# A routed feed-forward layer whose first products split 192 features as 128 + 64, with the first steps and the late slots of an audio tower re-ordered

## The chip, the cores and the metric

The kernel runs on one NeuronCore of a Trainium2 chip, in one launch. The metric is the device time of that launch in microseconds (us). Three timed runs of the kernel before gave 555.41, 556.99 and 558.28 us; the median is 556.99 us.

## What is computed

The input is 64 audio clips of 4000 samples, in float32. Seven 1-D convolutions (128 channels each, strides 5, 2, 2, 2, 2, 2, 2), each followed by a layer norm over channels and a GELU, leave 12 tokens per clip. Then come a projection to 192 features, one attention block with 6 heads, and a feed-forward layer with 9 experts:

```
h = x[:, None, :]
for w, g, b, s in zip(conv_ws, ln_gs, ln_bs, strides):
    h = gelu(layernorm(conv1d(h, w, s)) * g + b)
h = layernorm(h) * fln_g + fln_b;  h = h @ proj_w + proj_b          # (64, 12, 192)
h = h + attention(layernorm(h))
xt = layernorm(h).reshape(-1, 192)                                  # 768 tokens
prob = softmax(xt @ Ws + bs);  p, route = max(prob), argmax(prob)
out_e = gelu(xt @ W1[e] + b1[e]) @ W2[e] + b2[e]                    # 192 -> 768 -> 192
final = out_0 if route == 0 else p * out_route + (1 - p) * out_0
h = h + final
```

Expert 0 is computed for every token (the "common" expert), and each token's own expert for tokens that are sorted by expert first.

## The kernel before

**The tower.** The clips are taken in 8 groups of 8 (`NT = 8`). A group's layer outputs are cut into chunks `(layer, group, k)`. For a chunk PE does the convolution (`conv`, L790 to L801), ACT squares (L1474), DVE sums the squares (L1176), POOL takes the power -1/2 (L647), DVE scales (L1185), PE turns the result (`turn`, L820) and ACT applies GELU with scale and offset by channel (L1492, L1504). The order is written out by hand: `SLOTS` is a list of rows (chunk, jobs, preparations), made of `HEAD`, five repeated bodies, `LAST` and `DRAIN`. Every engine walks through the slots in the same order and does its own part of each; `STEPS`, filled from the tables `RUN_0` to `RUN_7`, puts the steps of a token group (projection, attention, routing) into slots. Each engine executes strictly in its own order, so a slot's order decides what waits behind what.

**The start.** The first layer's norm needs no convolution output: the variance of a window follows from a 10 x 10 Gram matrix of the centred taps. So before the first convolution: PE centres the taps (L1000), DVE repeats them (L1310), PE makes the Gram products (L1008), DVE masks and adds them into `gram` (L1316, L1319). PE turns the samples ("raw", L838, copied by DVE, L1101), and multiplies them with `gram` ("z", L849 to L853); DVE makes the variances (L1108 to L1113), POOL takes their power -1/2 in four parts (L641, 2.4 us each), DVE scales the samples (`scale`, L1140 to L1149), PE turns them ("xt", L863), DVE copies (L1164), PE multiplies by the first taps ("l0", L874, with `w0t` from L1326 to L1335) and ACT applies GELU (L1515). The other layers' taps are centred and turned on PE in four batches of four (`turn_taps`, L769) and kept by ACT (L1466).

**The feed-forward layer.** The 192 features of a token lie on partitions as two halves of 96, with a row of ones as 97th row of the second half, which carries the bias `b1`. A job `("up", p, f)` multiplies one of six blocks of 128 hidden features of expert 0 with the tokens of part p (`PARTS`: 288, 288, 96, 96 tokens). `up_tile(j)` does the same for a tile of sorted tokens (L1057 to L1061):

```
for f in range(NF):
    o = ps[:, 2 * b + f // 4, (f % 4) * P:(f % 4 + 1) * P]
    nc.tensor.matmul(o, w[0:DH, 0, f * P:(f + 1) * P], xst[0:DH, b, 0, :], start=True, stop=False)
    last = nc.tensor.matmul(o, w[:, 1, f * P:(f + 1) * P], xst[:, b, 1, :], start=False, stop=True)
```

ACT applies GELU (L1521), and jobs `("down", i)` multiply by `W2` (L895). When the last group's experts are known (`rank`, L991 to L995, then the chain of small DVE operations from L1380 on), the sorted tokens are worked off in 13 tiles of 128 (`NTILE`): load, turn (L1048, L1049), copy (L1414), `up_tile` (L1060, L1061), GELU over all 768 hidden features (`hidden`, L1580), `down_tile` (L1072), result (L1425, L1431) and an indirect store (L751). The expert's first weights are copied out by ACT ahead of its tile (`pick`, L1585), alternately into `xhl` and `watt`. PE's order there is: turn tile j+2, up tile j+1, down tile j. The first weights of experts 1 to 8 are loaded after the last convolution into the space that the layers' outputs held (L587 to L591).

## Time and profile before

| | us |
|---|---|
| median of three runs | 556.99 |
| the profiled execution, as timed | 555.56 |
| its span in the trace | 553.8 |
| PE busy | 527.0 (95% of the span) |
| ACT busy | 307.0 (55%) |
| DVE busy | 306.1 (55%) |
| POOL busy | 257.3 (46%) |

A busy PE means only that a matmul was in flight, since matmuls are pipelined. A float32 product appears in the trace as two weight loads (PEld) and two matmuls (PE), called two passes below; a turn (transpose) is one pass. The time from one start to the next says what a pass costs, not its duration. The span is 1.76 us shorter than the time of the same execution.

### The profile page before, as it was taken

Reading aid. Unit: us, or ns where it says so; the run is one execution under the profiler, and the core shown is the slowest. Engines: PE = TensorE matmul, PEld = TensorE weight load, DVE = VectorE, ACT = ScalarE, POOL = GpSimd, SP = SyncE. Lnnn points to the kernel's source line nnn. Section 1 sums busy time; section 2 is a strip of 40 time slices with the busy share of each in tenths; the row PEclk is TensorE's granted clock in tenths of the full one; section 3 lists DMA queues with packets and bytes.
Section 4 is the critical chain, followed back from the end, with each engine's and each line's share of the span. In section 5 each row is a group of like instructions: output and inputs, shape, how many; then the busy total and the mean of one; then the engine's idle time right before and its main releaser. Section 6 shows DMA issues by size and latency. Waiting matters only on the chain.

```text
span 553.8 us, 11088 instructions
## 1 busy us (share of the span) xinstructions
PE 527.0 (95%) x4043; PEld 496.1 (90%) x4043; DVE 306.1 (55%) x759; ACT 307.0 (55%) x557; POOL 257.3 (46%) x298
## 2 busy tenths in 40 slices
PE   6899999999999999999999999999999996799995
PEld 6797998899999999999999999899899885699995
DVE  4665564457566676766575666745564443612231
ACT  1566647656584766568565846763663423544440
POOL 5674564776239426743762494333242120034433
PEclk9999999999999999999999999999999996999999
DMA  6490001693000000000000000000000088151110
GB/s 173 121 311 10 1 8 24 172 234 89 19 2 17 14 19 7 20 20 7 2 20 20 8 20 1 20 7 1 2 8 5 1 210 206 35 151 46 51 34 11
DMA packets 19495, 29.45 MB, mean 53 GB/s; under 512 B 2611, under 2 KB 13837, under 8 KB 19443
## 3 DMA queue, kind: packets, MB, share of 16 engines
q1 hardware_dynamic: 16131, 18.95, 13.1%
q0 software_dynamic: 3296, 9.78, 7.1%
q8 instruction: 34, 0.56, 0.4%
q14 instruction: 18, 0.15, 0.1%
q10 hardware_dynamic: 16, 0.00, 0.0%
HBM read 17.09 MB, written 9.18 MB: 47 GB/s over the span
## 4 chain that ended last, share of the span: by engine, by line
PE 86%; DVE 4%; ACT 3%; POOL 2%; issue 2%; SPq 1%; DMA 1%; POOLq 0%; DVEq 0%; ACTq 0%
PE ps L801 22%; PE ps L793 11%; PE ps L790 8%; PE ps L820 7%; PE ps L1072 5%; PE ps L874 4%; PE ps L1061 3%; PE ps L1060 3%; PE ps L895 2%; PE ps L791 2%; PE ps L795 2%; PE ps L940 2%; PE ps L963 2%; PE ps L949 1%; PE ps L863 1%
## 5 line engine op out<-in xcount | busy, mean ns | idle before, releaser
L647 POOL TENSOR_TENSOR rstd<-ssum,neghalf 128x4 f32<-128x4 f32 (+9 forms) x128 | 114.7, 896 | 199.5 <-DVE ssum L1176 199.3
L801 PE MATMUL ps<-wt,wide 128*120 128x128 f32 (+3 forms) x1200 | 144.6, 274 | 1.5 <-ACT wide L1504 1.2
L1474 ACT ACTIVATE work<-ps 128x512 f32<-128x512 f32 (+9 forms) x128 | 65.3, 510 | 139.1 <-PE ps L795 71.9
L801 PEld LDWEIGHTS ps<-wt,wide 128*120 128x120 f32 (+3 forms) x1200 | 138.0, 181 | 5.0 <-issue 2.7
L1185 DVE TENSOR_TENSOR work<-ps,rstd 128x512 f32<-128x512 f32 (+9 forms) x128 | 74.2, 579 | 67.0 <-POOL rstd L647 63.6
L1176 DVE TENSOR_REDUCE ssum<-work 128x4 f32<-128x516 f32 (+9 forms) x128 | 73.6, 575 | 64.4 <-ACT work L1474 64.1
L641 POOL TENSOR_TENSOR rstd<-var,half 128x12 f32<-128x12 f32 (+3 forms) x39 | 78.9, 2036 | 8.3 <-DVE var L1113 7.7
L1515 ACT ACTIVATE h<-ps,lncol 128x512 f32<-128x512 f32 (+1 forms) x120 | 80.5, 717 | 2.5 <-PE ps L874 2.4
L793 PE MATMUL ps<-wt,h 128*128 128x256 f32 x288 | 70.1, 380 | 0.0
L820 PE MATMUL ps<-ident,work 128*128 128x128 f32 (+3 forms) x408 | 64.1, 269 | 2.2 <-ACT wide L1492 1.0
L1492 ACT ACTIVATE wide<-ps,lncol 128x256 f32<-128x256 f32 (+1 forms) x112 | 54.4, 539 | 2.1 <-PE ps L820 1.8
L793 PEld LDWEIGHTS ps<-wt,h 128*128 128x128 f32 x288 | 51.1, 191 | 4.9
L790 PE MATMUL ps<-wt,h 128*128 128x128 f32 x400 | 54.7, 277 | 0.3 <-ACT h L1515 0.3
L820 PEld LDWEIGHTS ps<-ident,work 128*128 128x128 f32 (+3 forms) x408 | 47.6, 141 | 4.7 <-DVE work L1185 2.3
L790 PEld LDWEIGHTS ps<-wt,h 128*128 128x128 f32 x400 | 50.5, 192 | 1.3 <-issue 0.5
L874 PE MATMUL ps<-cols,w0t 128*128 128x512 f32 (+1 forms) x120 | 43.9, 421 | 2.6 <-ACT h L1515 1.5
L1504 ACT ACTIVATE wide<-ps,lncol 128x448 f32<-128x448 f32 (+4 forms) x64 | 41.9, 655 | 2.0 <-PE ps L820 1.2
L1580 ACT ACTIVATE work<-ps 128x768 f32<-128x768 f32 x13 | 10.5, 811 | 35.4 <-PE ps L1061 32.7
L1072 PE MATMUL ps<-W2s,work 128*128 x156 | 27.7, 327 | 0.0
L751 POOL DMA_INDIRECT out_dram<-xnat,idt x13 | 13.1, 1010 | 30.9 <-DVE xnat L1431 30.3
L1414 DVE COPY xst<-ps 96x256 f32<-96x256 f32 x13 | 5.5, 421 | 37.1 <-issue 19.3
L1072 PEld LDWEIGHTS ps<-W2s,work 128*128 128x128 f32 x156 | 25.0, 190 | 0.3 <-issue 0.3
(238 smaller groups left out, 813.2 us busy)
## 6 DMA issues: line engine op xcount, KB each, us to landing
sorted_tokens<-zero POOLq DMA_DIRECT2D x1, 5886.5 KB, 30.7
W2s<-in_L_ffn_W_dram SPq DMA_DIRECT2D x9, 576.0 KB, 8.2
wide<-in_L_ffn_W_dram SPq DMA_DIRECT2D x8, 576.0 KB
cols<-cols SPq DMA_DIRECT2D x24, 128.0 KB, 2.2
cols<-sorted_tokens SPq DMA_DIRECT2D x13, 96.5 KB, 2.2
xnat<-in_x_dram SPq DMA_DIRECT2D x7, 130.0 KB, 2.6
wt<-in_L_ffn_b_dram SPq DMA_DIRECT2D x1, 864.0 KB, 4.5
wide<-in_L_tok_conv_w_dram SPq DMA_DIRECT2D x4, 192.0 KB, 2.9
```

The costliest lines, as they stand in the source:

```text
L641: gp.tensor_tensor(rstd0[:, lo:hi], var0[:, lo:hi], half0[:, lo:hi], ALU.pow).then_inc(s_pow, 1)
L647: gp.tensor_tensor(rstd[0:rows, idx, 0:count], ssum[0:rows, idx, 0:count], neghalf[0:rows, 0:count], ALU.pow).then_inc(rstd_done, 1)
L790: nc.tensor.matmul(y[:, j * C:(j + 1) * C], local(2 * (lo + j) + 1), wt[:, 0, :], start=(j == 0), stop=False)
L793: nc.tensor.matmul(y[:, (j - 1) * C:(j + 1) * C], local(2 * (lo + j)), wt[:, 1:3, :].rearrange("p t c -> p (t c)"), start=False, stop=False)
L801: last = nc.tensor.matmul(y[0:rows, j * C:(j + 1) * C], h[l - 1][g % 2][:, at:at + rows], wt[:, TAP0[l] + tap, :], start=(tap == 0), stop= ...
L820: last = nc.tensor.transpose(to, xh[0:rows, n % 2, j * C:(j + 1) * C], ident[0:rows, 0:rows])
L874: nc.tensor.matmul(o[:, 0:w], w0t[:, j, :], xcol[(QUADS * g + q) % XC][:, 0:w], start=True, stop=True).then_inc(j_done, 1)
L1072: last = nc.tensor.matmul(o, ht[:, b, f * P:(f + 1) * P], W2s[:, bass.ds(own, 1), f, :].rearrange("p e d -> p (e d)"), start=(f == 0), sto ...
L1176: nc.vector.reduce_sum(ssum[0:rows, n % 4, 0:count], sq[0:rows, n % 2, 0:count, :], axis=X).then_inc(ssum_done, 1)
L1185: nc.vector.tensor_tensor(xh[0:rows, n % 2, 0:w].rearrange("p (j c) -> p j c", c=C), ybank(n)[0:rows, 0:w].rearrange("p (j c) -> p j c", c=C),
L1474: nc.scalar.activation(sq[0:rows, n % 2, 0:CUTS[l][k], 0:C], ybank(n)[0:rows, 0:w].rearrange("p (j c) -> p j c", c=C), ACT.Square).then_in ...
L1515: nc.scalar.activation(dst, src, ACT.Gelu, bias=lncol[:, 8:9], scale=lncol[:, 0:1]).then_inc(j_act, 1)
```

## The change

1. **Layout.** Of the 192 features, block f of the first half (f < 3) uses features 0 to 127 as one full product of 128 rows and features 128 to 191 as a product of 64 rows, which lie on partitions 64 to 127. Block f + 3 uses features 64 to 191 as the full product and 0 to 63, on partitions 0 to 63, as the product of 64 rows. The 64-row products of f and f + 3 follow each other and use different halves of the array and different PSUM banks. So six blocks take 6 full products and 3 pairs, where they took 12 products.
2. **Bias.** `b1` leaves the products. It is turned into columns once (`b1col`), and ACT adds it in the GELU. In the tiles, where a block's bias is a column of its own, the one GELU over 768 columns becomes six over 128; the picked weights have 1158 columns on 128 partitions where they had 1536 on 97. The routing bias `bs` is added by DVE, one more operation a group.
3. **Loads.** The first weights of each expert come in two loads, and two more bring the 64-row parts of all eight; the two one-partition loads of the bias go. Tap loads go ahead of the second load of samples.
4. **Start.** Gram products go ahead of the raw turn, `gram` ahead of its copy, the variance products ahead of the turned taps; the last two batches of taps are turned between the first steps of layer 0.
5. **Slots.** `up` jobs go in twos (f, f + 3); `LAST`, `DRAIN` and `RUN_5` to `RUN_7` are rewritten.

```diff
+DR = D - P
+NH2 = NF // 2
+HALF1 = DFF // 2
+WIDE1 = DFF + HALF1
+EW = WIDE1 + NF
...
 DRAIN = [
-    (None, [('up', 0, 0), ('up', 0, 1)], []),
+    (None, [('up', 0, 1)], []),
     ((2, 7, 0), [], []),
-    ((2, 7, 1), [], []),
+    ((2, 7, 1), [('up', 0, 0)], []),
...
+    (None, [('down', 1), ('down', 2)], []),
     (None, [('down', 0)], []),
...
-                nc.tensor.matmul(o[:, 0:(hi - lo) * M], W1c[0:DH, 0, f * P:(f + 1) * P], xt[0:DH, 0, cols], start=True, stop=False)
-                nc.tensor.matmul(o[:, 0:(hi - lo) * M], W1c[:, 1, f * P:(f + 1) * P], xt[:, 1, cols], start=False, stop=True)\
-                    .then_inc(j_done, 1)
+                w = (hi - lo) * M
+                nc.tensor.matmul(o[:, 0:w], W1c[:, f * P:(f + 1) * P], xt[:, f // NH2, cols], start=True, stop=False)
+                if f >= NH2:
+
+                    at = DFF + (f - NH2) * P
+                    nc.tensor.matmul(jbank(JOB[job] - 1)[:, 0:w], W1c[DR:P, at:at + P], xt[DR:P, 1, cols],
+                                     start=False, stop=True).then_inc(j_done, 1)
+                    nc.tensor.matmul(o[:, 0:w], W1c[0:DR, at:at + P], xt[0:DR, 0, cols], start=False, stop=True).then_inc(j_done, 1)
...
                 for f in range(NF):
-                    o = ps[:, 2 * b + f // 4, (f % 4) * P:(f % 4 + 1) * P]
-                    nc.tensor.matmul(o, w[0:DH, 0, f * P:(f + 1) * P], xst[0:DH, b, 0, :], start=True, stop=False)
-                    last = nc.tensor.matmul(o, w[:, 1, f * P:(f + 1) * P], xst[:, b, 1, :], start=False, stop=True)
+                    nc.tensor.matmul(block(f), w[:, f * P:(f + 1) * P], xst[:, b, f // NH2, :], start=(f % NH2 == 0), stop=False)
+                for f in range(NH2):
+                    at = DFF + f * P
+                    nc.tensor.matmul(block(f), w[DR:P, at:at + P], xst[DR:P, b, 1, :], start=False, stop=(f == NH2 - 1))
+                    last = nc.tensor.matmul(block(f + NH2), w[0:DR, at:at + P], xst[0:DR, b, 0, :], start=False, stop=(f == NH2 - 1))
...
             pe.wait_ge(s_w0, 16)
             nc.tensor.matmul(ps[:, 0, 0:K0], centre[:, :], w0nat[:, :], start=True, stop=True).then_inc(s_w0p, 1)
-            pe.wait_ge(s_pads, 3)
-            job_raw(("raw", 0))
-            pe.wait_ge(s_w0k, 1)
-            nc.tensor.matmul(ps[:, 7, 0:C], h[2][1][:, 8 * C:9 * C], centre[:, :],
-                             start=True, stop=True).then_inc(s_w0p, 1)
             pe.wait_ge(s_w0k, 2)
...
-            turn_taps(0)
+            pe.wait_ge(s_pads, 3)
+            job_raw(("raw", 0))
+            nc.tensor.matmul(ps[:, 7, 0:C], h[2][1][:, 8 * C:9 * C], centre[:, :],
+                             start=True, stop=True).then_inc(s_w0p, 1)
             for job in HEAD[1][1]:
                 job_z(job)
+            turn_taps(0)
             turn_taps(1)
-            turn_taps(2)
-            turn_taps(3)
...
                 if step == "choose":
                     ve.wait_ge(t["lo"], r + 1)
-                    nc.vector.reduce_max(best[:, 0:1], pb[0:M, 0:NE], axis=X).then_inc(t["top"], 1)
+                    nc.vector.tensor_tensor(lg[:, :], pb[0:M, 0:NE], bsr[:, :], ALU.add).then_inc(t["lg"], 1)
...
-                nc.scalar.activation(ht[:, b, :], ps[:, 2 * b:2 * b + 2, :].rearrange("p k c -> p (k c)")[:, 0:DFF],
-                                     ACT.Gelu).then_inc(e_act, 1)
+                ac.wait_ge(e_pick, j + 1)
+                for f in range(NF):
+                    last = nc.scalar.activation(ht[:, b, f * P:(f + 1) * P], ps[:, 2 * b + f // NH2, f % NH2 * P:(f % NH2 + 1) * P],
+                                                ACT.Gelu, bias=W1r[b][:, WIDE1 + f:WIDE1 + f + 1])
+                last.then_inc(e_act, 1)
```

**How it moves instructions.** Three places. The lines are those of each program. First PE at the very start; `centre,wide` products of 128x128 in fours are batches of turned taps. Before:

```order
L838 MATMUL ps<-ident,xnat 128x128 x3
L1004 MATMUL ps<-centre,wide 128x128
L1008 MATMUL ps<-wide 128x10 x2
L769 MATMUL ps<-centre,wide 128x128 x4
L849 MATMUL ps<-gram,xwin 128x240
L852 MATMUL ps<-gram,xwin 128x240
L853 MATMUL ps<-gram,xwin 128x30
L769 MATMUL ps<-centre,wide 128x128 x12
L1019 MATMUL ps<-ident,lnraw 128x16
L863 MATMUL ps<-ident,xhl 128x128 x4
L874 MATMUL ps<-cols,w0t 128x512 x3
```

With the change:

```order
L1052 MATMUL ps<-wide 128x10 x2
L876 MATMUL ps<-ident,xnat 128x128 x3
L1057 MATMUL ps<-centre,wide 128x128
L887 MATMUL ps<-gram,xwin 128x240
L890 MATMUL ps<-gram,xwin 128x240
L891 MATMUL ps<-gram,xwin 128x30
L807 MATMUL ps<-centre,wide 128x128 x8
L1065 MATMUL ps<-ident,lnraw 128x16
L901 MATMUL ps<-ident,xhl 128x128 x4
L807 MATMUL ps<-centre,wide 128x128 x4
L912 MATMUL ps<-cols,w0t 128x512 x2
L807 MATMUL ps<-centre,wide 128x128 x4
```

The variance products (`gram,xwin`) no longer stand behind a batch of taps, and eight of the sixteen tap turns stand behind the first turn of layer 0.

Second, PE in the last token group, from its keys and scores (`kpad,qs`) to its second turn. Before (L895 is ("down", 5), L963 the attention values, L971 the output projection, L883 and L884 one block of ("up", 2, 4)):

```order
L949 MATMUL ps<-kpad,qs 96x288 x2
L955 MATMUL ps<-ident,t 96x96 x6
L883 MATMUL ps<-xt,wide 128x96
L884 MATMUL ps<-xt,wide 128x96
L963 MATMUL ps<-vv,t 96x32 x6
L901 MATMUL ps<-ident,xn 96x96
L902 MATMUL ps<-ident,xn 96x96
L971 MATMUL ps<-watt,act 96x192
L972 MATMUL ps<-watt,act 96x192
L895 MATMUL ps<-W2s,h 96x192 x6
L901 MATMUL ps<-ident,xn 96x96
L902 MATMUL ps<-ident,xn 96x96
```

With the change (L938 is ("down", 5), L945 and L946 the second turn):

```order
L998 MATMUL ps<-kpad,qs 96x288 x2
L938 MATMUL ps<-W2s,h 96x192 x6
L1004 MATMUL ps<-ident,t 96x96 x6
L1012 MATMUL ps<-vv,t 96x32 x6
L949 MATMUL ps<-ident,xn 96x96
L950 MATMUL ps<-ident,xn 96x96
L1020 MATMUL ps<-watt,act 96x192
L1021 MATMUL ps<-watt,act 96x192
L945 MATMUL ps<-ident,xn 128x96
L946 MATMUL ps<-ident,xn 128x96
```

("down", 5) went from behind the output projection to behind the scores, and nothing of expert 0 is left between the turned probabilities and the second turn.

Third, PE in one tile of sorted tokens, with the change:

```order
L945 MATMUL ps<-ident,cols 128x128
L946 MATMUL ps<-ident,cols 128x128
L1112 MATMUL ps<-xst,xhl 128x128 x6
L1115 MATMUL ps<-xst,xhl 128x128
L1116 MATMUL ps<-xst,xhl 128x128
L1115 MATMUL ps<-xst,xhl 128x128
L1116 MATMUL ps<-xst,xhl 128x128
L1115 MATMUL ps<-xst,xhl 128x128
L1116 MATMUL ps<-xst,xhl 128x128
```

L1112 are the full products, L1115 those of partitions 64 to 127, L1116 those of partitions 0 to 63. Before, twelve products L1060, L1061 stood there in turn.

## Rows read from the trace of the kernel before

**Rows 1.** The page: the chain that ended last, share of the span by engine.

```profile
PE 86%; DVE 4%; ACT 3%; POOL 2%; issue 2%; SPq 1%; DMA 1%; POOLq 0%; DVEq 0%; ACTq 0%
```

**Rows 2.** Windows: us, then PE, PEld, DVE, ACT, POOL busy, PEclk, DMA share, GB/s.

```profile
100.00:200.00 100.00, 98.55 (x783) 93.53 (x782) 62.24 (x144) 61.88 (x119) 56.76 (x66) 1.00 0.32 76
...
470.00:480.00 10.00, 8.20 (x56) 7.37 (x54) 5.80 (x32) 4.35 (x9) 0.95 (x1) 0.87 0.03 7
...
465.00:469.30 4.30, 3.54 (x11) 2.90 (x12) 1.19 (x4) 0.32 (x1) 0.22 (x2) 0.50 0.91 206
...
484.52:543.30 58.78, 58.78 (x467) 58.42 (x467) 15.41 (x47) 25.02 (x23) 24.85 (x26) 1.00 0.25 69
```

**Rows 3.** Timeline of the start: start us, length, what [idle before, and who ended it].

```profile
3.19 0.43 DVE L1310 COPY wide<-ps 128x260 f32<-128x260 f32 x1 [0.38 <-PE ps L1000]
...
4.92 0.56 DVE L1101 COPY xwin<-ps 128x384 f32<-128x384 f32 x1 [1.31 <-PE ps L838]
...
5.10 0.87 PE L1008 MATMUL ps<-wide 128*128 128x10 f32 x4
...
6.76 0.41 DVE L1319 TENSOR_TENSOR gram<-xsc 128x240 f32<-128x240 f32 x1
...
7.69 2.05 PE L769 MATMUL ps<-centre,wide 128*128 128x128 f32 x8 [1.72 <-DMA wide<-in_L_tok_conv_w_dram]
...
9.53 1.01 PE L849 MATMUL ps<-gram,xwin 128*128 128x240 f32 x2
...
11.71 9.71 POOL L641 TENSOR_TENSOR rstd<-var,half 128x12 f32<-128x12 f32 x4 [5.73 <-DVE var L1113]
...
13.16 0.58 ACT L1466 COPY wt<-ps 128x512 f32<-128x512 f32 x1 [2.81 <-PE ps L769]
...
15.96 0.66 PE L863 MATMUL ps<-ident,xhl 128*128 128x128 f32 x4 [0.33 <-DVE xhl L1149]
...
18.02 2.11 ACT L1515 ACTIVATE h<-ps,lncol 128x512 f32<-128x512 f32 x3 [1.92 <-PE ps L874]
...
20.67 1.05 PE L790 MATMUL ps<-wt,h 128*128 128x128 f32 x8
```

**Rows 4.** Timeline of PE around its one product on 16 rows.

```profile
14.95 0.52 PE L769 MATMUL ps<-centre,wide 128*128 128x128 f32 x3
15.40 0.23 PE L1019 MATMUL ps<-ident,lnraw 16*128 16x16 f32 x1
```

**Rows 5.** Timeline of PE in a tile of sorted tokens.

```profile
487.52 0.39 PE L1060 MATMUL ps<-xst,watt 96*128 96x128 f32 x2
487.75 0.39 PE L1061 MATMUL ps<-xst,watt 97*128 97x128 f32 x2
```

**Rows 6.** Groups of the whole trace by form, ACT: count, busy us, mean ns.

```profile
L1515 ACT ACTIVATE h<-ps,lncol 128x128 f32<-128x128 f32 x24 | 10.0, 456 | 0.0
...
L1580 ACT ACTIVATE work<-ps 128x768 f32<-128x768 f32 x13 | 10.5, 811 | 35.4 <-PE ps L1061 32.7 <-issue 2.7
L1585 ACT COPY xhl<-wide 97x1536 f32 x7 | 10.3, 1467 | 0.8 <-issue 0.7
```

**Rows 7.** The chain in order of time: start us, us on it; part 0 or 1.

```profile
438.22 0.49 PE ps L883 x2
```

**Rows 8.** Timeline from the last group's scores on.

```profile
461.37 0.70 PE L955 MATMUL ps<-ident,t 96*96 96x96 f32 x6 [2.35 <-ACT t L1541]
...
462.73 2.11 PE L963 MATMUL ps<-vv,t 96*96 96x32 f32 x12 [0.21 <-DVE t L1261]
...
467.70 4.05 PE L895 MATMUL ps<-W2s,h 128*96 128x192 f32 x12
...
469.86 0.38 DVE L1199 TENSOR_SCALAR xn<-acc,mv,rs 96x192 f32<-96x192 f32 x1 [0.95 <-POOL rs L654]
...
471.54 0.37 PE L901 MATMUL ps<-ident,xn 96*96 96x96 f32 x1
...
480.64 2.16 PE L895 MATMUL ps<-W2s,h 128*96 128x192 f32 x12 [0.43 <-ACT h L1521]
```

More of the change, by code:

```diff
@@ L224, with blocks @@
     (None, [], []),
+    (None, [], []),
+    (None, [], []),
+    (None, [], []),
+    (None, [], []),
+    (None, [], []),
 ]
 SLOTS = HEAD + [row for g in range(2, NT - 1) for row in body(g)] + LAST + DRAIN
-AFTER = [('down', 6), ('up', 3, 0), ('up', 3, 1), ('up', 3, 2), ('up', 3, 3), ('up', 3, 4), ('up', 3, 5), ('down', 7)]
+AFTER = [('down', 6), ('up', 3, 0), ('up', 3, 1), ('up', 3, 2), ('down', 7)]
+def blocks(jobs):
+    return [k for j in jobs for k in ([j, (*j[:2], j[2] + NH2)] if j[0] == "up" else [j])]
+SLOTS = [(c, blocks(jobs), prep) for c, jobs, prep in SLOTS]
+LATER = blocks(AFTER)
 LAG = 2
@@ L234 @@
 NG = len(CHUNKS)
-JOBS = [j for row in SLOTS for j in row[1]] + AFTER
+JOBS = [j for row in SLOTS for j in row[1]] + LATER
 JOB = {j: n for n, j in enumerate(JOBS)}
@@ L267 @@
             assert slot_of(("xt", g_ - 1, (1 if g_ < PAIRED_FROM else 0, 2 if g_ == PAIRED_FROM else 4)[q_])) <= part_
+POWS = [p[1:] for row in SLOTS for p in row[2] if p[0] == "pow"]
+for g_ in range(NT):
+    for c_ in scale_cuts(g_)[1:]:
+        done_ = next(n for n, c in enumerate(pow_cuts(g_)) if c >= c_)
+        at_ = sum(len(pow_cuts(b)) - 1 for b in range(g_))
+        assert sorted(POWS[at_:at_ + done_]) == [(g_, i) for i in range(done_)]
 STEPS = [[] for _ in SLOTS]
```

186 lines of the change are left out of this document (106 added, 80 removed).

## The prediction

> **What bounds the kernel now.** I read the chain that ended last first: 86% of it is PE, no other engine has over 4% [rows 1]. So what PE issues counts, and a wait counts where PE has nothing else. Next the windows, for where this holds. From 28 us to 440 us PE hardly pauses: it is busy 98.55 of 100 us in a typical stretch [rows 2]. In the tiles of sorted tokens it never pauses, 58.78 of 58.78 us, with ACT at 25.02 and POOL at 24.85 [rows 2]. Between lie two stretches where the reader should see waits: the start, where PE's products have holes and the chain runs through DVE and POOL [rows 3], and the last token group, where each step waits for the one before [rows 8] and the granted clock is 0.50, that is 1.2 of 2.4 GHz [rows 2]. The change touches all four, so I cost them one by one, against the profiled execution's 555.56 us; that is 1.43 below the median of 556.99. Half a per cent, 2.8 us, is about what a measurement of this kernel can tell from no change.
>
> **The start.** Before, the variance products begin at 9.53, though `gram` stands ready at 6.76 + 0.41 = 7.17: they are queued behind eight turned-tap passes, which wait for their load until 7.69 [rows 3]. In the change the Gram products (at 5.10 before) can start once DVE has copied their operand, at 3.19 + 0.43 = 3.62. With the 2.07 from their start to `gram` as before, it is ready near 5.75; the raw copy (0.56), behind `gram` on DVE now, ends near 6.35. The variance products then start at about 6.4, 3.1 earlier, and POOL's first power, 2.18 behind their start, at 8.6. A part of it takes 9.71 / 4 = 2.43; the first turn came 15.96 - 14.14 = 1.8 behind its end, with 0.7 of that for DVE's tap products in between, so it comes near 12.2. Against that, ACT now keeps two batches of taps (0.58 each) between its first three GELUs. They start 2.06 behind the first turn and take 2.11, so they end at 20.13 before; now they start near 14.6 (0.3 more for DVE's last tap product) and end, with 1.2 in between, at 17.9 [rows 3]. The first convolution (20.67 before) follows: **-2.2 us**. The second sample load, passed by five tap loads, is wanted only behind the first two convolutions, so its lateness is hidden. Bounds: -3.4 if the kept taps hide in waits, -1 if the second layer's taps land late and hold PE behind `turn_taps(1)`. PE is the bound behind, so the gain is carried on.
>
> **A pair of 64-row products.** The trace of before holds none. Its nearest rows: a product of 128 moving columns costs 487.75 - 487.52 = 0.223, in two passes of 0.111 [rows 5]; one of 288 columns 0.485 [rows 7]. At best a pair costs one product, at worst two. I take the middle that the order of starts suggests: matmuls start in program order in every row; the two passes of a product need the same half of the array; so only the second pass of one and the first of the next can run together. Three pairs in a row are then 7 pass times where six products take 12, and a lone pair 3 instead of 4. To this comes the change of array shape. The only one in the trace is the 16-row product at 15.40: its predecessors start at 14.95, 15.06 and 15.17 (three, one pass apart), so it stands 0.23 behind the last one, 0.12 more than a pass [rows 4]. I take 0.12 for each change of shape, two per group of pairs; bounds 0 and 0.3 (two passes last 0.39, so one lasts 0.28, 0.17 more than its pass time, and the next load, of at least a pass time, isn't ahead).
>
> Here a rule can be weighed. The Trainium skill (TensorEngine Tiling (Array Packing), Key Properties) says that a change of tiling mode drains the array, and that tiles work independently. The row at 15.40 agrees with the first in size; nothing in this trace shows the second. By the page alone, with a pair at one product and switches as above, the tiles' term below would be -5.6 instead of -4.1.
>
> **The tiles.** 13 tiles of six blocks: 12 products x 0.223 = 2.67 become 6 x 0.223 + 7 x 0.111 = 2.11, and two switches add 0.24: -0.32 a tile, **-4.1 us** (-8.7 at one product a pair and free switches; +7.8 with no overlap and dear switches). The turns now load 128 instead of 96 columns, still within a pass of 0.11: 0. ACT's part of a tile grows from 0.81 to six GELUs of at most 0.46 (the row of 128x128, which has scale and offset by pointer), 2.7; the pick shrinks with its columns from 1.47 to about 1.15 [rows 6]. Together 3.9. PE's stretch of 58.78 holds 13 ups, 11 turns of 0.22 and 11 downs [rows 2], so a down is 1.97 and a tile 4.85, now 4.53: more than ACT's. And down j waits for GELU j behind down j-1, a turn and an up of 2.3: hidden. If PE fell to 4.2 it would still hide. Only the last tile has no next up as cover: 2.7 less 1.97 less what it waited before: **+0.5** (0 to +0.8).
>
> A second rule: the Trainium skill (ScalarE: Activation LUTs, What ACT_TABLE_LOAD costs) states that each pointer operand adds about 93 ns to an ACTIVATE. By it one of the six takes some 0.37 instead of 0.46 and ACT's part of a tile 3.4; neither would reach PE's time.
>
> **Jobs of expert 0.** Parts 0 and 1, on busy PE: six lone pairs, each a pass of 0.243 less, -1.5; twelve switches at 0.12, +1.4. **0** (-2.9 to +3.6). Parts 2 and 3 lie among waits. Their GELUs have an offset, but no more instructions than before.
>
> **The last group.** ("down", 5) stood between the output projection and the second turn, 4.05 long at the low clock, and the turn (471.54) waited for it although its input was ready at 469.86 + 0.38 = 470.24 [rows 8]. It now fills the hole of 2.35 before 461.37. The turn's next releaser is that normalization: -1.2. The routing bias and the copied bias columns add two DVE operations of 0.2 to the chain: +0.4. A hole filled may keep the clock high for the values (2.11 at 1.2 GHz), up to -2 more; but with less work until the ranks the low clock may last over ("down", 6) and the jobs behind it, which cost 4.05 against 2.16 at 2.4 GHz [rows 8]: up to +2. Net **-1.0** (-3.3 to +1.5). The loads of the first weights, 18 instead of 10 on SP's queue and of the same bytes, cost nothing: the DMA share falls from 0.91 to 0.03 by 470 to 480 [rows 2], and the first pick stands behind the last jobs of expert 0, whose last down starts at 480.64 [rows 8]; that is some 10 us of cover, and without it each us late would be one lost. SP's token loads wait for the scatter, not for these.
>
> **Sum:** -2.2 - 4.1 + 0.5 + 0 - 1.0 = -6.8: 548.8 against the profiled 555.56, about **549**.
>
> **Rivals.**
> - *Loads in single file, slightly dear.* PEld is busy 58.42 of 58.78 us in the tiles [rows 2]: if weight loads of the two halves can't overlap, 128-column loads pace the pairs and nothing is won there, while switches stay: 13 x 0.24 + 1.4 = +4.5, with -2.2, +0.5 and -1.0 it makes 557.4. The point from which it decides: loads over half a pass each. For it: a pass costs 0.111 whether load or matmul is looked at. Against: the two halves lie on different partitions.
> - *Switches drain PE (the slower side).* Each tile leaves and re-enters the full array. If each change costs 0.3 and leaves nothing to overlap: 13 x 0.6 + 12 x 0.3 = +11.4, less 2.7 for the rest: 564. If pairs overlap all the same: 13 x (0.6 - 0.56) + 3.6 - 1.5 = +2.6, about 555.5. The point from which the tiles lose is 0.28 a switch. For it: only one cheap switch was seen, and into a 16-row product. Against: it cost 0.12.
> - *Full overlap.* A pair costs one product: tiles -5.6, jobs -1.5, in all 546. For it: nothing here; against: starts in order.
> - *The drain gives back.* The clock stays at 1.2 GHz into ("down", 6): 548.8 + 2.5, 551.
> - *The pairs aren't side by side*, since both sit on the same banks: excluded, f and f + 3 go to different ones.
>
> **Chances.** Forecast 0.42, full overlap 0.14, drain gives back 0.12 (these three faster: 0.68); single file 0.14; overlap with dear switches 0.08; no overlap and dear switches 0.06; something late in the rewritten slots, +3 and more, 0.04. Single file lies 0.3% up and is mostly within 0.5%: same 0.20, slower 0.12. The range reaches from the full-overlap case with cheap switches and a warm drain (543) to the single-file case (557.5) with a little over it.
>
> **What would show it.** In the changed profile: first convolution at 18.5 (right: 17.5 to 19.5); starts of L1115 and L1116 in a tile: seven pass times for three pairs, 0.78, against 1.33 for single file and 0.67 for full overlap; a step of 0.2 to 0.25 at the first L1115 and at the first product behind L1116; tiles 4.53 apart instead of 4.85; ACT's idle before L1647 still ended by PE; the last group's second turn released by DVE's normalization. The forecast is wrong if tiles are over 4.75 apart, or if ACT or a late load becomes PE's releaser in the tiles.

## The result, and the profile after

| | before | after |
|---|---|---|
| median, first set of runs (9 and 9) | 555.95 us | 553.38 us |
| ratio, with 95% interval | | 0.9941 (0.992 to 0.9962) |
| median, second set (11 and 6) | 557.05 us | 553.03 us |
| ratio, with 95% interval | | 0.9931 (0.9911 to 0.9952) |
| profiled execution, as timed; span | 555.56; 553.8 us | 554.60; 552.8 us |

By the ratios the changed kernel is 0.6 to 0.7% faster, some 3.3 to 3.8 us, about half of the 6.8 that the sum gave; the medians of the two sets differ by 2.6 and by 4.0, so the figure is known to about 1 us. The second set was run beside the last experiment and is told of there. One thing to keep in mind for every reading of the clock below: the profiled execution of the kernel before had a mean granted clock of 0.988, while its 62 executions beside the experiments had 0.976 to 0.987, with a median of 0.984. Its profile thus shows less of the low clock than is usual for it.

The page of the changed kernel, busy times and the chain by engine [rows 1]:

```profile
PE 525.6 (95%) x4044; PEld 487.4 (88%) x4044; DVE 306.4 (55%) x768; ACT 313.5 (57%) x620; POOL 257.1 (47%) x298
...
PE 88%; ACT 3%; DVE 3%; POOL 3%; issue 2%; DMA 0%; POOLq 0%; ACTq 0%; DVEq 0%
```

PE still sets the end. The start, in the timeline (start us, length, what, idle before and who ended it), against [rows 3]:

```profile
6.40 1.17 PE L887 MATMUL ps<-gram,xwin 128*128 128x240 f32 x2 [0.57 <-DVE xwin L1156]
...
8.75 9.52 POOL L679 TENSOR_TENSOR rstd<-var,half 128x12 f32<-128x12 f32 x4 [2.77 <-DVE var L1168]
...
12.22 0.66 PE L901 MATMUL ps<-ident,xhl 128*128 128x128 f32 x4 [0.34 <-DVE xhl L1204]
...
18.09 1.05 PE L828 MATMUL ps<-wt,h 128*128 128x128 f32 x8
```

The variance products come at 6.40 instead of 9.53, the first turn at 12.22 instead of 15.96, the first convolution at 18.09 instead of 20.67: 2.6 earlier. That is still so for the layer 0 products at 119.00 (121.59 before), and 2.2 are left from 129.55 (131.75 before) on. That gain does not reach the end of the convolutions. The last reduction of a convolution chunk on DVE, before and then after:

```profile
445.31 0.28 DVE L1176 TENSOR_REDUCE ssum<-work 96x1 f32<-96x129 f32 x1
```

```profile
444.78 0.28 DVE L1231 TENSOR_REDUCE ssum<-work 96x1 f32<-96x129 f32 x1 [0.50 <-ACT work L1535]
```

It is 0.53 earlier, not 2.15. The windows of PE from 400 to 445 us say where the rest went (stretch, PE busy, granted clock, DMA share, GB/s), before and then after:

```profile
400.00:445.00 45.00, 44.95 (x347) 1.00 0.02 4
```

```profile
400.00:445.00 45.00, 42.65 (x319) 1.00 0.02 4
```

PE is busy in all but 0.05 of the 45 us before, and in all but 2.35 now: it idles 2.30 more. The last group of the kernel before, by the rows that neither [rows 8] nor the text ahead shows:

```profile
449.91 2.12 PE L895 MATMUL ps<-W2s,h 128*96 128x192 f32 x12
...
457.84 1.18 PE L949 MATMUL ps<-kpad,qs 96*96 96x288 f32 x4 [0.94 <-DVE kpad L1231]
...
474.03 0.34 PE L991 MATMUL ps<-hot,upper 96*96 96x9 f32 x2 [0.97 <-DVE hot L1287]
...
474.73 2.17 PE L895 MATMUL ps<-W2s,h 128*96 128x192 f32 x12
...
483.30 0.29 PE L1048 MATMUL ps<-ident,cols 128*96 128x128 f32 x1 [0.49 <-issue]
```

These are ("down", 4), the scores, the first of the rank products, ("down", 6) and the first tile's turn. The later stretch in the changed kernel, by windows:

```profile
450.00:456.00 6.00, 6.00 (x32) 0.72 1.06 374
456.00:462.00 6.00, 5.06 (x36) 1.00 1.09 235
462.00:468.00 6.00, 4.03 (x29) 0.93 0.44 96
468.00:474.00 6.00, 2.05 (x9) 0.50 0.00 0
474.00:480.00 6.00, 6.00 (x24) 0.50 0.04 12
```

And the last group's timeline, against [rows 8]:

```profile
450.67 3.50 PE L938 MATMUL ps<-W2s,h 128*96 128x192 f32 x12
...
460.71 2.12 PE L938 MATMUL ps<-W2s,h 128*96 128x192 f32 x12
463.22 0.70 PE L1004 MATMUL ps<-ident,t 96*96 96x96 f32 x6 [0.40 <-ACT t L1603]
464.58 1.19 PE L1012 MATMUL ps<-vv,t 96*96 96x32 f32 x12 [0.65 <-DVE t L1317]
...
470.97 0.42 PE L945 MATMUL ps<-ident,xn 96*128 96x96 f32 x1 [2.37 <-DVE xn L1254]
...
475.24 4.13 PE L938 MATMUL ps<-W2s,h 128*96 128x192 f32 x12
483.62 2.16 PE L938 MATMUL ps<-W2s,h 128*96 128x192 f32 x12 [0.75 <-ACT h L1582]
486.28 0.30 PE L945 MATMUL ps<-ident,cols 128*128 128x128 f32 x1 [0.49 <-issue]
```

("down", 5) fills the hole at 460.71, and the second turn at 470.97 is released by DVE's normalization, as forecast. But ("down", 4) takes 3.50 and ("down", 6) 4.13, where they took 2.12 and 2.17 before: the clock is at 0.50, 1.2 GHz, over most of the first and all of the second. The first tile's turn stands at 486.28, 2.98 later than before (483.30). The tiles then win it back:

```profile
487.64 1.50 PE L1112 MATMUL ps<-xst,xhl 128*128 128x128 f32 x12
489.07 0.37 PE L1115 MATMUL ps<-xst,xhl 64*128 64x128 f32 x1
489.08 0.37 PE L1116 MATMUL ps<-xst,xhl 64*128 64x128 f32 x1
489.28 0.27 PE L1115 MATMUL ps<-xst,xhl 64*128 64x128 f32 x1
489.29 0.27 PE L1116 MATMUL ps<-xst,xhl 64*128 64x128 f32 x1
489.39 0.27 PE L1115 MATMUL ps<-xst,xhl 64*128 64x128 f32 x1
489.40 0.27 PE L1116 MATMUL ps<-xst,xhl 64*128 64x128 f32 x1
...
489.73 0.27 PE L1115 MATMUL ps<-xst,xhl 64*128 64x128 f32 x1
489.74 0.27 PE L1116 MATMUL ps<-xst,xhl 64*128 64x128 f32 x1
489.94 0.33 PE L945 MATMUL ps<-ident,cols 128*128 128x128 f32 x1
```

The two 64-row passes of a pair start together, six times, 0.11 apart after the first: a pair costs one product. There are larger steps, of 0.2 where a pass alone makes 0.11, between the first and the second pass and behind the last. An up takes 2.30 (487.64 to 489.94), from 2.67; tiles stand 4.575 us apart, from 4.85. So the profile's books are: last convolution -0.5, first tile +3.0, end of the span -1.0.

### The profile page after: what moved, and what is told of

The parts are those of the page before. It is cut to its first block, busy times and chain, and to the rows that moved or that the text cites. A ratio compares the mean times of both kernels' runs of the same rounds, so it can differ in the third digit from the quotient of the medians.

```text
span 552.8 us, 11176 instructions
## 1 busy us (share of the span) xinstructions
PE 525.6 (95%) x4044; PEld 487.4 (88%) x4044; DVE 306.4 (55%) x768; ACT 313.5 (57%) x620; POOL 257.1 (47%) x298
## 4 chain that ended last, share of the span: by engine, by line
PE 88%; ACT 3%; DVE 3%; POOL 3%; issue 2%; DMA 0%; POOLq 0%; ACTq 0%; DVEq 0%
PE ps L839 22%; PE ps L831 11%; PE ps L828 8%; PE ps L858 7%; PE ps L1127 5%; PE ps L912 4%; PE ps L1112 3%; PE ps L938 3%; PE ps L829 2%; PE ps L833 2%; PE ps L989 2%; PE ps L1115 2%; PE ps L922 2%; PE ps L1012 1%; PE ps L901 1%
## 5 line engine op out<-in xcount | busy, mean ns | idle before, releaser
L1565 ACT ACTIVATE wide<-ps,lncol 128x480 f32<-128x480 f32 (+4 forms) x64 | 42.1, 657 | 4.6 <-PE ps L858 3.9
L1475 DVE COPY xst<-ps 128x256 f32<-128x256 f32 x13 | 5.5, 425 | 33.9 <-PE ps L946 33.9
L912 PEld LDWEIGHTS ps<-cols,w0t 128*128 128x128 f32 x120 | 20.1, 190 | 4.2 <-ACT h L1576 3.1
```

The source lines that it names most:

```text
L912: nc.tensor.matmul(o[:, 0:w], w0t[:, j, :], xcol[(QUADS * g + q) % XC][:, 0:w], start=True, stop=True).then_inc(j_done, 1)
```

## The experiments

The rows of PE between 400 and 445 us, the granted clock in the last group and the start of the first tile's turn are read in each. In all nine variants that have the changed tiles the last tile's GELUs also start late in the profile, which costs 0.7 us in e4_grouped and 1.3 in the others; the changed kernel's own two profiles don't show it. e11_tiles_filled tells more of it. A comparison of such a variant's time with the changed kernel's holds this on top. Their ratios go by the same kernel before, whose medians were 556.5 to 557.1 in these runs.

**e1_start_only.** The kernel before with the start of the change alone (order of PE, DVE and ACT there, and the load that five tap loads pass).

> The kernel before with the change's start alone (order of Gram, raw, variance products and turned taps, loads of taps ahead of the second samples). Theory A (the gain of the start is carried through a PE-bound kernel to the end): first convolution 2.6 us earlier as in the changed kernel, span 2.1 to 2.6 us shorter, ratio 0.9955. Rival B (the last token group, a chain of waits, swallows what comes earlier): first convolution earlier all the same, span within 1 us of before, ratio over 0.998.

Measured: 554.62, ratio 0.996 (0.9945 to 0.9974). The last convolution came 2.15 earlier and the kpad scores too (455.69 for 457.84), the rank products 3.05 earlier (470.98), but the first tile's turn only 0.41 (482.89). The windows tell why:

```profile
462.00:468.00 6.00, 5.08 (x21) 0.53 0.74 167
468.00:474.00 6.00, 4.62 (x26) 0.76 0.00 0
474.00:480.00 6.00, 5.81 (x32) 0.67 0.17 45
```

and in its timeline ("down", 6):

```profile
472.20 4.13 PE L895 MATMUL ps<-W2s,h 128*96 128x192 f32 x12
```

The clock fell a second time, over ("down", 6) and the first up jobs behind it, which in the kernel before ran at full clock. So the start is worth what was forecast where it is made, and in this profile the last group's clock took most of it back. Over the runs 2.2 are left: most other executions had a mean granted clock of 0.986 or 0.987, where this one had 0.981. Neither the tiles nor the new slots are needed for a low clock over ("down", 6): the last group is here that of the kernel before.

**e2_old_slots.** The changed kernel with the kernel before's LAST, RUN_5 to RUN_7 and DRAIN, its up jobs halved in number and each paired:

```
 DRAIN = [
-    (None, [('up', 0, 1)], []),
+    (None, [('up', 0, 0)], []),
     ((2, 7, 0), [], []),
-    ((2, 7, 1), [('up', 0, 0)], []),
+    ((2, 7, 1), [], []),
...
```

> The changed kernel with the slot tables of before (LAST, RUN_5 to RUN_7 and DRAIN, where each two of the single up jobs become one pair). Theory A (the rewritten late slots lose what they were meant to win, because the pairs leave holes and the clock falls twice, in the last token group): last convolution at about 442 instead of 443.8, granted clock falls once, first tile's turn at 482 to 484 instead of 486.3, time 2 to 4 us below the changed kernel, ratio 0.987 to 0.991. Rival B (the losses come with the pairs themselves, whatever the slots): first tile's turn at 486 or later, ratio 0.994 or above.

Measured: 556.14, ratio 0.9986 (0.9974 to 0.9998), slower than the changed kernel. PE is still idle between 400 and 445 us, though less:

```profile
400.00:445.00 45.00, 43.38 (x331) 1.00 0.02 4
```

Of it 0.63 is a wait of the probabilities' turns for ACT, 0.55 one of the logits, 0.30 one of a convolution's turn. So the new table is not the only cause of the holes: of the 2.30 more than before, 1.57 remain with the old one. Theory A failed in the rest too, and rival B's figures were met within 0.02 us (first tile's turn at 485.98). The old table has ("down", 5) back in its old place, behind the output projection (468.46); it costs 2.96 there, the chain from the scores to the ranks takes 16.39 (457.28 to 473.67), and ("down", 6) takes 4.13 all the same.

**e3_down5_late.** One job moved, five slots later, behind the last group's values:

```
     (None, [], []),
-    (None, [('down', 5)], []),
+    (None, [], []),
...
+    (None, [('down', 5)], []),
```

> The changed kernel with the one job down 5 moved back to where it stood before (behind the output projection of the last group, slot 49 instead of 44). Theory A (with that job early, PE is nearly idle before the last ranks and down 6 runs at the low clock; with it late, the clock is back for down 6): the last group's second turn 1 to 2 us later than 470.97, down 6 2.2 us long instead of 4.1, first tile within 0.7 us of 486.3, ratio as the changed kernel within 0.002. Rival B (the move is a plain gain of 2 us): 2 us slower than the changed kernel, ratio 0.997 to 0.999.

The edit does not do what was expected of it: the job comes to stand behind the values and ahead of the heads' turn, while in the kernel before it stood behind the output projection. That place is the one of e2_old_slots.

Measured: 559.52, ratio 1.0048 (1.0032 to 1.0063), some 6 over the changed kernel. Its timeline:

```profile
461.99 0.70 PE L1004 MATMUL ps<-ident,t 96*96 96x96 f32 x6 [2.35 <-ACT t L1603]
463.35 2.11 PE L1012 MATMUL ps<-vv,t 96*96 96x32 f32 x12 [0.66 <-DVE t L1317]
465.27 4.13 PE L938 MATMUL ps<-W2s,h 128*96 128x192 f32 x12
```

With the hole of 2.35 left open, the clock is low by the values (2.11 instead of 1.19), ("down", 5) costs 4.13 where it stands in the chain ahead of the heads' turn, and ("down", 6) still takes 4.13. The first tile's turn comes at 488.71, 4.0 behind that of the changed kernel's second profile (484.69), and 1.3 are the late GELUs. This is the price of an empty hole and a job in the chain, not that of the old place. What the old place costs is read from e2_old_slots: a chain of 16.39 instead of 14.48 in the changed kernel's second profile, 1.9 us.

**e5_filled.** The changed kernel with products that compute nothing in the last group's holes (an extra product of the identity with itself into a free bank; everything else is computed as before):

```
+            def filler(n):
+                for _ in range(n):
+                    nc.tensor.matmul(ps[:, 2, 0:P], ident[:, :], ident[:, :], start=True, stop=True)
+
+            FILL = {"turn_probs": 2, "values": 2, "turn_heads": 1, "out_project": 8, "turn_2": 1, "logits": 4}
```

> The changed kernel plus 18 products of ident with ident into a free PSUM bank, in the holes of PE between the last group's turned probabilities and its ranks; their results are read by nobody. Theory A (what the last group loses is the low clock): granted clock 1.0 from 461 to 480, output projection 0.5 us instead of 0.9 a product, down 6 2.1 us instead of 4.1, first tile's turn at 482.5 to 484 instead of 486.3, 2 to 3.5 us below the changed kernel, ratio 0.987 to 0.991. Rival B (the group waits on DVE, ACT and POOL, and PE's clock hardly matters): first tile within 1 us of 486.3, ratio 0.993 to 0.997; if the fillers come in the way of the chain, above that.

Measured: 552.27, ratio 0.9925 (0.99 to 0.9949). The clock stays at 1.00 until 478, ("down", 6) takes 2.17, the first tile's turn is at 483.12, 3.16 before that of the changed kernel's first profile and 1.57 before that of its second. A fall over ("down", 7) (3.56) is left. The intervals of the ratios overlap, so in time alone this gain is not shown.

**e4_grouped.** In a tile's up, the three 64-row products of rows 64 to 127 first, then the three of rows 0 to 63:

```
                     nc.tensor.matmul(block(f), w[DR:P, at:at + P], xst[DR:P, b, 1, :], start=False, stop=(f == NH2 - 1))
+                for f in range(NH2):
+                    at = DFF + f * P
                     last = nc.tensor.matmul(block(f + NH2), w[0:DR, at:at + P], xst[0:DR, b, 0, :], start=False, stop=(f == NH2 - 1))
```

> The changed kernel, but in a tile's first FFN product the three 64-row products of rows 64 to 127 stand first and the three of rows 0 to 63 behind them, instead of alternating. Theory A (the array starts products in program order, and overlap needs a neighbour on the other half of the rows): only the last pass of the first group overlaps the first pass of the second, 11 steps in the place of 6; with 0.11 us a step that is +0.55 us an up, 13 ups, +7.2 us: about 560.5 against 553.4 of the changed kernel, and a tile every 5.12 us instead of 4.575. Rival B (a product starts as soon as its half of the rows is free, past those ahead of it): nothing changes, 553 to 554, a tile every 4.575.

Measured: 558.17, ratio 1.0022 (1.0006 to 1.0038); tiles 4.90 us apart. Between the two theories:

```profile
487.31 0.60 PE L1115 MATMUL ps<-xst,xhl 64*128 64x128 f32 x3
487.64 0.37 PE L1118 MATMUL ps<-xst,xhl 64*128 64x128 f32 x1
487.75 0.27 PE L1115 MATMUL ps<-xst,xhl 64*128 64x128 f32 x1
487.86 0.27 PE L1118 MATMUL ps<-xst,xhl 64*128 64x128 f32 x1
487.86 0.27 PE L1115 MATMUL ps<-xst,xhl 64*128 64x128 f32 x1
```

L1118 is the line of the second group. Its first pass starts at 487.64, ahead of the fourth pass of the first group at 487.75. So a start in program order, on which my sum rested (and "each engine executes strictly in its own order", as far as starts on different rows go), is wrong. But three passes of the first group run alone and only two steps hold a pass of each: the twelve passes take ten steps, where theory A had eleven and the changed kernel has six. An up costs 0.32 more. The products start past some that are ahead of them; how many they could pass was not tried.

**e6_single.** The changed kernel with expert 0's ups in single file (a full product, then its own 64-row product), in the slots of the kernel before:

```
+                at = DFF + f % NH2 * P
+                rows, k = (slice(DR, P), 1) if f < NH2 else (slice(0, DR), 0)
+                nc.tensor.matmul(o[:, 0:w], W1c[rows, at:at + P], xt[rows, k, cols], start=False, stop=True).then_inc(j_done, 1)
```

> The changed kernel with expert 0's first products one after another, each with its own 64-row product behind its full product (no pair), in the slots and places of the kernel before; start and tiles stay changed. Theory P (the pairs are what costs before the last conv: a pair holds both job banks, so the next pair waits for two GELUs): the gaps of TensorE over 0.2 us between 400 us and the last conv, 2.1 us in all in the changed kernel and none before, are gone; the single 64-row products cost a switch each way, 0.1 to 0.2 us an up, some 15 to 18 ups before the last conv, so the last conv stands at -2.2 + 1.5 to 3 us against before. Theory T (the rewritten slot tables cost it): also no gaps, but then the kernel with the old slots and pairs should have had none either, and it had. Rival S (a 64-row product in single file costs much more than a 96-row one): up rows visibly longer than 0.243 us a pass and time above 558. With the last group as before (low clock into down 6 or not) the time is 553 to 557.

Measured: 564.3, ratio 1.0129 (1.0104 to 1.0154); the profiled execution was the shortest, at 560.06. The holes are gone (PE busy 45.00 of 45.00), which speaks for theory P; but rival S was right too:

```profile
482.40 0.46 PE L925 MATMUL ps<-xt,wide 64*128 64x96 f32 x2
482.79 0.46 PE L922 MATMUL ps<-xt,wide 128*128 128x96 f32 x2
```

An up of 96 columns takes 0.78, where the kernel before takes 0.445 (its four passes at 0.11): each change of shape costs 0.17. With 288 columns an up takes 1.36 (439.33 to 440.69) instead of 0.98, 0.19 a change. Such longer ups also cover more of each wait, so the missing holes don't single out the pair; e10_tiles_only, without pairs and without longer ups, does that better.

**e8_filled_more.** The filled kernel with ten fillers in its longest hole and some ahead of the scores, ahead of ("down", 7) and between the first two tile turns.

> The changed kernel with the filler products of the run before (2, 2, 1, 8, 1, 4 of them in the last group's gaps) and more: 10 instead of 8 in the longest gap, 3 ahead of the scores, 3 ahead of down 7, 2 between the first two tile turns. Theory C (what ate the gain is the granted clock falling to 0.5 over dense work of the last group): the profile shows 1.00 from 440 to 490, down 6 and down 7 at 2.1 to 2.2 us each, the first tile's turn at 481.5 to 482.5 and 551 or less (span 549.5 to 550). Rival D (the fillers stand in the way of the chain): the first tile's turn no earlier than 483.1 and the time 552 or more.

Measured: 551.63, ratio 0.991 (0.9888 to 0.9931), the clock 1.00 from 440 to 490 us, ("down", 6) and ("down", 7) 2.17 and 2.16, the first tile's turn at 481.38. The clock and the place are as theory C had them; the time missed its figure by 0.6. Whether the clock is what ate the gain is decided by the next run, not by this one.

**e9_before_filled.** The kernel before, its holes filled in the same way.

> The kernel before with filler products in the same gaps of the last group (3 ahead of the scores, 9 behind them, 1, 2, 1, 1, 4 further on, 2 ahead of down 7, 2 between the tile turns). Theory C: the low stretch of 462.8 to 472.3 goes, and with it the 1.9 us that down 5 took more, the 0.7 of the head products and 0.3 of rank and logits: first tile's turn at about 480.3 instead of 483.3 and 553.5 to 554 against 556.6. The change in its filled form then gains what the start and the tiles are worth less the waits of the pairs: -2.2 - 4.0 + 1.7 = -4.5. Rival D: fillers bring nothing here, 556 to 557, and the clock's fall in the changed kernel is no cause of its missing gain.

Measured: 553.40, ratio 0.994 (0.9918 to 0.9962). The first tile's turn here, and then in e8_filled_more:

```profile
479.56 0.28 PE L1064 MATMUL ps<-ident,cols 128*96 128x128 f32 x1 [0.49 <-issue]
```

```profile
481.38 0.30 PE L945 MATMUL ps<-ident,cols 128*128 128x128 f32 x1 [0.49 <-issue]
```

So fillers alone, with nothing of the change, win as much as the change does. The second forecast of this run failed: between the filled kernels the change gains 1.8 us (553.40 to 551.63), not 4.5, and its first tile's turn is 1.8 later. The low clock cost the kernel before as much as the changed one, so it is not what made the change fall short.

**e10_tiles_only.** The changed kernel's start and tiles; expert 0, the logits and all slot tables as before (W1 of expert 0 in two halves of 96 rows with its bias as row 97).

> The changed kernel with its start and its tiles (first product split 128 + 64, pairs, six GELUs, biases in columns), but expert 0, the logits and the slot tables as in the kernel before (96 + 97 rows, two products an up). Theory P (pairs and split of expert 0 are worth nothing in time and cost about 1.7 us before the last conv): last conv at 442.1 to 442.3 as in the start-only kernel, tiles every 4.575 us, and the sum is -2.0 (start, measured) - 4.0 (tiles): 550.6. Rival Q (the last group gives back what comes earlier, whatever it is, through the clock): 552 to 554, with down 6 or down 7 at over 3 us.

Measured: 551.77, ratio 0.9903 (0.9879 to 0.9927). PE never idles before 445 us and the last convolution is at 442.12, 2.2 earlier than before:

```profile
400.00:445.00 45.00, 44.95 (x340) 1.00 0.04 14
```

Theory P holds as to the place. The time is 1.2 over its figure: ("down", 6) takes 3.85 us at the low clock, and the last tile's GELUs are late by 1.33.

**e11_tiles_filled.** That kernel with fillers (3 ahead of the scores, 9 behind them, 1, 2, 1, 1, 4 further on, 2 ahead of ("down", 7), 2 between the tile turns).

> The run before this one with the filler products of the filled kernel before, in the same gaps. Theory C and P together: 553.4 (kernel before, filled) - 2.0 (start) - 4.0 (tiles) = 547.4, granted clock 1.00 throughout the last group, first tile's turn at 477.4, some 4 us under the filled changed kernel. Rival R (the gain of the filled kernels comes from one and the same source as the tiles' or the start's and does not add): 549.5 or more.

Measured: 548.84, ratio 0.985 (0.9819 to 0.9881), clock 1.00 in the last group, first tile's turn at 478.02. It leaves nothing of the computation out and beats both kernels: 1.5% under the one before, 0.8% under the changed one. It adds to 1.4 us less than theories C and P together said; 1.3 of that stand at the end of its profile:

```profile
536.08 1.66 ACT L1650 ACTIVATE work<-ps,xhl 128x128 f32<-128x128 f32 x6 [4.29 <-remote]
537.88 2.21 PE L1133 MATMUL ps<-W2s,work 128*128 x12 [1.30 <-ACT work L1650]
```

The last tile's GELUs start about 1.7 after their products, and the last down waits 1.30. In the changed kernel's own profile they don't (the downs follow each other, 24 passes in 4.17). Of the nine variants with the changed tiles eight show the late start in their profile and one half of it, the two profiles of the changed kernel none. What ACT waits for there the trace names only as remote; it stays open, and no run was made on it.

**e12_one_hole.** The changed kernel with ten fillers behind the out-projection only.

> The changed kernel with 10 filler products behind the last group's out-projection alone (its longest gap, 2.37 us). In the profile of the changed kernel the clock fell at 466.8, ahead of that gap. Theory E (the fall comes from the gaps ahead, 459 to 467, and once fallen the clock comes back through dense work): still a fall at about 467, the fillers run at 0.5 and bring the clock back before down 6, which takes 2.2 to 3 us instead of 4.1; first tile's turn 484 to 485 and 551.5 to 552.5. Theory F (the long gap alone keeps it down): no low stretch at all, first tile's turn at 483 and 551 to 552. Rival G: nothing gained, 553 to 554, fillers at half speed delay the second turn to 471.5 or later.

Measured: 554.65, ratio 0.9963 (0.9942 to 0.9985), if anything slower; the interval overlaps those of the changed kernel. The clock had fallen ahead of the hole, so the ten products took 4.47 at half speed and the second turn came at 471.42, behind them; it came back by 471.5 and fell again over ("down", 6), 3.77. Rival G came nearest: in this run fillers behind the fall brought nothing, while the same hole filled together with those ahead of it (e5_filled) kept the clock up.

**e13_after_again.** The changed kernel itself, once more.

> The changed kernel itself once more, beside the same kernel before, so that its ratio stands in the same conditions as those of the variants. Theory P (the change's expert-0 half costs 1.6 us net): ratio 0.994 to 0.995, 553.3 to 554 where the kernel before is at 556.6, against 0.990 of the variant with tiles and start only. Rival (the two sets of runs differ, not the kernels): ratio 0.990 to 0.992. In its profile: PE idle by about 2.3 us between 400 and 445 us again; the clock's falls need not lie where they lay; the last tile's GELUs late by up to 1.7 us in this profile as in most variants, or not.

Measured: 553.03, ratio 0.9931 (0.9911 to 0.9952), span 551.2. PE is busy 42.65 of 45 us again. The early fall over ("down", 4) does not recur, nor is it in any variant: the kpad scores stand at 458.38 instead of 459.69, the first tile's turn at 484.69 instead of 486.28. The later fall is there (0.50 from 465 to 475), and ("down", 6) runs into it. The interval overlaps a little with that of e10_tiles_only, so "expert 0 is better left alone" rests on the medians (0.9931 and 0.9903) and on the rows of 400 to 445 us.

## Why the prediction was half right

The profiles give the account: from 553.8 to 551.2 us, the span of the changed kernel's second profile, are -2.6, where the sum had -6.8. The step that failed is "Jobs of expert 0: **0**", with "parts 2 and 3 lie among waits" put at nothing: it counted products, and left out what pairs do to the waits around them. That cost 1.6 to 1.8 us ahead of the last convolution and about as much behind it, in the stretch that the last group's term forecast at -1.0.

**Start, -2.2.** Right in every link: 6.40 for about 6.4, 8.75 for 8.6, 12.22 for 12.2, 18.09 for about 18.5; -2.15 at the last convolution of e1_start_only, and its ratio makes -2.2. That the total fits so well is in part luck: the first convolution gained 0.4 more than the forecast, and as much was lost again between 119 and 130 us, which the sum did not hold.

**Tiles, -4.1, and last tile, +0.5.** From the first turn to the last downs the second profile of the changed kernel takes 541.02 - 484.69 = 56.33, the kernel before 543.42 - 483.30 = 60.12: -3.8. The size is right, by errors that cancel. "Matmuls start in program order" and the seven pass times for three pairs are wrong: the pairs take six, full overlap, as the rival had it. But an excursion, the way from the full array to 64 rows and back, costs 2.30 - 18 x 0.111 = 0.30 an up instead of 0.24, and a down takes 2.05 instead of 1.96. The page TensorEngine Tiling (Array Packing), Key Properties, of the Trainium skill was right on both counts, independent tiles (a pair's passes start within 0.01 us) and a drain at a change (the larger steps); the figure that I worked out from it, -5.6, is too good since the drain costs more than one row had shown. The six GELUs take 1.66, not up to 2.7, so the last tile costs nothing in the two profiles of the changed kernel (from the last downs to the end 10.18 and 10.19, from 10.38) and 1.3 where they start late.

The other rule (ScalarE: Activation LUTs, What ACT_TABLE_LOAD costs, of the Trainium skill: a pointer operand adds about 93 ns) is borne out in kind: a GELU of 128 x 128 takes 456 with two pointers [rows 6] and 375 to 376 with one. Here it is 81 ns, and the measured figure counts.

**Jobs of expert 0, 0.** This term failed, by +1.6 to +1.8 (the last convolution is 0.5 and 0.3 earlier in the two profiles, not 2.15). The time of the products alone is as summed or better: a pair of ups of 288 columns takes 1.75 (437.99 to 439.74) instead of 1.96. But I counted only products. PE is without work for 2.35 of 45 us in the changed kernel, 1.62 with the old table and pairs (e2), 0.05 with neither (e10). The waits that the changed kernel's rows show there add up to 2.26: 0.65 for kpad, 0.51 and 0.23 in the convolutions' chain, 0.41 of the logits, 0.18 of a turn, and only 0.28 for the GELU of a pair. That last one is the pair's own doing, since it holds both job banks until two GELUs have read them; it, and the like one behind this stretch:

```profile
440.40 1.24 PE L922 MATMUL ps<-xt,wide 128*128 128x288 f32 x4 [0.28 <-ACT h L1582]
448.96 0.69 PE L922 MATMUL ps<-xt,wide 128*128 128x96 f32 x4 [0.42 <-ACT h L1582]
```

The other waits are those of a chain's steps for their own inputs. My reading is that ups of one block used to stand before them, one here and one there, and that a pair fills one place where two ups filled two; e10_tiles_only fits it, but no run shows it by itself. How the 2.30 divide between the banks, the places and the table is not settled: a third job bank was not tried, because the other banks are in use there.

**Last group, -1.0.** This term failed by its sign: from the last convolution to the first tile's turn, +1.7 in the second profile and +3.5 in the first, where ("down", 4) alone took 1.3 more (3.50 for 2.19). The filled kernels take the low clock out of both sides. The stretch by its parts (differences of starts of the last convolution products, of the scores, of the first rank product and of the first tile's turn):

| us | before | changed, second profile | before, filled (e9) | changed, filled (e8) |
|---|---|---|---|---|
| last convolution to scores | 13.52 | 14.39 | 13.53 | 14.40 |
| scores to ranks | 16.19 | 14.48 | 12.88 | 13.09 |
| ranks to first tile's turn | 9.27 | 11.83 | 9.26 | 9.96 |
| together | 38.98 | 40.70 | 35.67 | 37.45 |

Each column is one profile. By them the low clock takes 3.3 in both kernels. In the changed one it takes less ahead of the ranks, since ("down", 5) stands in the hole and the values run at full clock, and more behind them, over ("down", 6) and the first ups. So the "up to -2" and "up to +2" that I let cancel did cancel. Rival "drain gives back" had the second of them right (+2.6 from ranks to turn), but not that the first would come with it.

What the term lacked is seen at full clock: +1.8 where -1.2 + 0.4 was forecast. Ahead of the scores it is +0.87 and behind the ranks +0.70. In each of the two stretches stand three pairs of 96 columns, each about 1.01 us long (480.78 to 481.79) for the 0.89 of two ups before. Behind the ranks that is +0.36; the rest there is waits, as that of 0.75 of ("down", 7) for two GELUs, which was 0.43. Ahead of the scores the three pairs take 3.0 us where the kernel before had five ups, 2.2; its sixth stood in the hole of the chain (461.91), where it cost next to nothing. In the chain between, +0.21 is the routing bias (the ranks wait 1.17 for DVE, where they waited 0.97). The -1.2 of ("down", 5) is not there at full clock: in the filled kernel before it stands in its old place and takes 2.12, and the second turn behind it waits 0.42 for DVE all the same.

With that the gap between the filled kernels is accounted for as well. Start and tiles are worth 6 us. Off go 2.2 ahead of the last convolution, which stands at 443.93 against 443.89 although the start is 2.15 earlier, 1.8 behind it, and 1.3 for the late GELUs of e8's profile. That leaves 0.7, and the two spans differ by 0.6 (550.1 and 549.5). The medians are 1.8 apart; in three of the six executions of e9 the clock was lower, 0.991 to 0.994. In time, filling gains 1.4 to 1.75 on the changed kernel and 3.2 on the kernel before; the late GELUs, which the filled changed kernel has in its profile and the changed one has not, are the greater part of that difference.

## What to carry to other kernels

Weigh an excursion of TensorE, full array to 64 rows and back, as a whole. Here it costs 0.3 to 0.35 us beside its passes however long it is: it pays where it holds many paired products (six pass times of 0.11 saved in a tile's up) and loses where it holds one pair of short ones (two passes of 0.11 saved for 0.35).

When a low clock is suspected of taking a gain, take it away on both sides, before and after. Filling only the changed kernel seemed to show the cause; filling the kernel before too showed that the clock cost both the same 3.3 us. And look whether the one profile that serves as "before" is a usual execution: here its clock was above that of all 62 others.

A change that makes work in a busy engine shorter but coarser has to be costed by its waits too: read the idle time of the busy engine in the stretch before and after (0.05 and 2.35 of 45 us), not only the sum of product times.

## What the runs showed of the hardware

- Two float32 passes of 64 rows on different halves of the array start within 0.01 us of each other, and a pair of 128 columns costs 0.11 per pass, as one alone. They needn't be neighbours in the program: in e4_grouped the second group's first pass started at 487.64, the first group's fourth, which is ahead of it in the program, at 487.75.
- A change between 128 and 64 rows costs 0.17 us at 96 columns and 0.19 at 288 in single file; in a tile's up the seams of one excursion add up to 0.30.
- Products that compute nothing were worth 3.2 us on the kernel before, 1.4 to 1.75 on the changed one and 2.9 on e10_tiles_only, where the granted clock was 1.00 over the last group's waits; ten of them behind the fall of the clock gained nothing (ratio 0.9963 against 0.9931 and 0.9941).
- Six GELUs of 128 x 128 with a bias pointer, each 376 ns, follow each other so closely that six take 1.66.
